# Slot table computed early, first group's chain reordered, bias added tile by tile, and constant matmuls on TensorE: an attention and mixture-of-experts kernel

## The chip, the cores and the metric

The kernel runs on one core of a Trainium2 chip. The metric is the device time of one execution in microseconds; lower is better. Engines are named as the profile names them: PE is TensorE (PEld its weight loads), DVE is VectorE, ACT is ScalarE, POOL is GpSimd, SP is the engine that issues most of the plain transfers.

## The reference

Input x has 16 sequences of 256 tokens with 128 features, in float32. All arithmetic is float32.

```python
x = x + attn(layernorm(x))      # 16 heads of 8; q and k divided by their norms; no softmax:
                                # out = (q k^T / 256**sigmoid(m)) v, then Wo and bo
x = x + ffn(layernorm(x))       # 8 experts, hidden size 512
# ffn: probs = softmax(x Wg^T); the two largest are taken
#      h = gelu(x w1[e] + b1[e]); eo = h w2[e] + b2[e]; out = sum of gate * eo over the two experts
```

## The kernel before

The 4096 tokens are 32 tiles of 128, in 8 groups of four tiles (`G = 4`, `NG = 8`); a group is two sequences. The kernel has three stages.

**Stage 1, attention and routing.** Every engine runs through `for n in STEPS` (n from -2 to 13) and calls a fixed, hand-written list of small functions, each for one group, such as `keys_of_x(n)` or `places(n - 2)`. Each engine works its list strictly in that order. A function begins with waits on semaphores and ends with an increment, so the lists mesh as a software pipeline. The life of group g:

- DVE takes statistics of x (`stats_of_x`, L832), ACT writes the normalised tile (`normalised`, L705), PE turns it (`turn_x`, L501), ACT copies it out (`turned_x`, L682), PE projects to q and k (`project`, L511). ACT squares them (`squares`, L694), DVE sums the squares (`sums_of_squares`, L881), clips them (`bounded`, L886), ACT takes the root (`norms`, L717), DVE inverts it (`inverse_norms`, L891) and scales q and k (`unit_qk`, L896).
- PE forms x^T k (`keys_of_x`, L529), ACT copies (`keys`, L699), PE multiplies by Wv (`values`, L545), DVE masks by heads (`heads`, L903), PE multiplies by Wo and by the router's weights (`out_weights` on PE, L552), ACT copies the product (`out_weights` on ACT, `gm`, L722), and PE applies it to q (`attend`, L561). DVE adds the residual (`attended`), whose bias part POOL wrote beforehand into `x2` (L443).
- DVE picks the two largest router values (`largest`, `where_largest`). PE counts how many earlier tokens go to each expert (`places` on PE, L570 to L574, into `psPos`, which shares a bank with the product `psGM`), DVE turns the counts into row numbers (`places` on DVE, L962 to L974), ACT writes the normalised rows (`rows`, L674). POOL scatters each tile twice with an indirect transfer into `xs` (L456), 64 transfers in all, in order of groups.

Step n of ACT begins with `out_weights(n - 2)`. PE's `places(n - 2)` waits for `s_gm >= n`, which means the copy of group n - 1. That copy is the first entry of ACT's step n + 1, behind `norms(n)`.

Between these, the expert weights are prepared, one expert per step: PE `centre_w1` (L474, L476), DVE `centred_w1` (L980), ACT `high_w1`, `high_w2` (L727, L732), DVE `low_w1`, `low_w2` (L985, L991).

After all steps PE sums the counts, DVE builds the table of slots (L1028 to L1048: which rows of `xs` each of 71 tiles of 128 rows starts at, and its expert), SP and ACT write eight blocks of padding (L337).

**Stage 2, experts.** A loop over 71 slots loads 128 rows (SP, L388 reads the row number into a register, L389 issues the load), turns them, runs both layers and scatters the results into `ys` (POOL, L463).

**Stage 3.** The two results of each token are read back, weighted and added to `x2`, and written out.

Of the kernel before, what the change touches and what calls it, by code (L numbers as in the profile page):

```python
# [19 lines left out]
P = 128  # L20
# [4 lines left out]
ALU = mybir.AluOpType  # L25
ACT = mybir.ActivationFunctionType
AX = mybir.AxisListType.X
# [4 lines left out]
def moe_block(nc, x, Wq, bq, Wk, bk, Wv, bv, Wo, bo, m, Wg, w1, b1, w2, b2, out, xs, ys):  # L32
# [8 lines left out]
    G = 4  # L41
# [17 lines left out]
    with ExitStack() as ctx:  # L59
# [284 lines left out]
        def _(sp):  # L344
# [32 lines left out]

            pads(sp, range(E // 2), s_pad)
            sp.wait_ge(s_tab, 1)
            sp.wait_ge(s_pad, 16 * (E // 2 + 1))  # L380
            sp.wait_ge(s_pad2, 16 * (E - E // 2))
# [4 lines left out]
            def load(s, b, i, e):  # L386
                after(sp, s_back[b], 16 * i)
                r = sp.value_load(rtab[0:1, bass.ds(s, 1)], min_val=0, max_val=E * REGION)  # L388
                sp.dma_start(xt[:, b, :], xs[bass.ds(r, P), :]).then_inc(s_xt[b], 16)  # L389
# [13 lines left out]
        def _(pool):  # L403
# [34 lines left out]
            for c in range(3):  # L438
                pool.wait_ge(s_xin[c], 16)
                n = G if c < 2 else NT - 2 * G  # L440
                t0 = c * G
                for q in range(t0, t0 + n, G):
                    pool.tensor_tensor(x2[:, q:q + G, :], xin[:, q:q + G, :],  # L443
                                       bobc[:].unsqueeze(1).to_broadcast([P, G, D]), ALU.add).then_inc(s_xb, 1)

# [25 lines left out]
        def _(pe):  # L471
            def centred(dst, src, bias):
# [4 lines left out]
                return mm  # L477

            pe.wait_ge(s_zero, 2)
            pe.wait_ge(s_const, 2)  # L480
# [7 lines left out]
            centred(psG[:, 0:E], wgT[:], None).then_inc(s_pw, 1)  # L488
            pe.wait_ge(s_w, 3)
            pe.wait_ge(s_ws, 3)  # L490
            pe.matmul(psKV[:, 0:E], woT[:], wgT[:], start=True, stop=True)
            pe.matmul(psKV[:, E:2 * E], borep[:], wgT[:], start=True, stop=True).then_inc(s_pw, 1)

            def turn_x(g):
# [82 lines left out]
            def centre_w1(e):  # L577
                if 0 <= e < E:
                    pe.wait_ge(s_wb, 32)
                    after(pe, s_w1, e)  # L580
                    centred(psQ[:], w1s[:, e, :], b1row[0:1, e, :]).then_inc(s_psW, 1)

            for n in STEPS:
                centre_w1(n - 3)
                out_weights(n - 1)
                turn_x(n + 1)
                places(n - 2)
                attend(n - 1)
                share_of_x(n)
                keys_of_x(n)  # L590
                project(n + 1)
                turn_q(n)
                values(n)

            pe.wait_ge(s_seen, NG)
            pe.wait_ge(s_pos, NG)
            pe.matmul(psCnt, ones[:, 0:1], seen[:], start=True, stop=True).then_inc(s_cnt, 1)


# [61 lines left out]
        def _(act):  # L661
# [130 lines left out]
        def _(dve):  # L792
# [195 lines left out]
            def low_w2(e):  # L988
                if 0 <= e < E:
                    dve.wait_ge(s_w2h, e + 1)  # L990
                    dve.tensor_tensor(w2p[:, e, :, 1, :], w2s[:, e, :].rearrange("p (c d) -> p c d", c=FC),  # L991
                                      w2p[:, e, :, 0, :].bitcast(F32), ALU.subtract).then_inc(s_w2l, 1)

            for n in STEPS:
                scale_and_shift(n - 1)
# [25 lines left out]
            links = [0]  # L1021

            def chain(ins):
                links[0] += 1
                ins.then_inc(s_tb, 1)
                dve.wait_ge(s_tb, links[0])
            dve.wait_ge(s_cnt, 1)
            dve.tensor_tensor(ptab[:], psCnt, regbase[0:1, 0, :], ALU.add).then_inc(s_ptab, 1)  # L1028
            chain(dve.tensor_scalar(cnti[:], psCnt, float(P - 1), None, ALU.add))
            chain(dve.tensor_scalar(tilesi[:], cnti[:], P.bit_length() - 1, None, ALU.logical_shift_right))  # L1030
            chain(dve.tensor_copy(tiles[:], tilesi[:]))
            dve.tensor_tensor_scan(tend[:], onee[:], tiles[:], 0.0, ALU.mult, ALU.add)
            chain(dve.tensor_scalar(tinc[:], tiles[:], -float(P), float(REGION), ALU.mult, ALU.add))
            chain(dve.tensor_tensor(past[:], sidx[:].unsqueeze(2).to_broadcast([1, NS, E]),
                                    tend[:].unsqueeze(1).to_broadcast([1, NS, E]), ALU.is_ge))
            dve.tensor_reduce(esum[:], past[:], AX, ALU.add)
            chain(dve.tensor_tensor(pinc[:], past[:], tinc[:].unsqueeze(1).to_broadcast([1, NS, E]), ALU.mult))
            dve.tensor_scalar(etabf[0:1, 1:1 + NS], esum[:], float(E - 1), None, ALU.min)
            chain(dve.tensor_reduce(rsum[:], pinc[:], AX, ALU.add))
            for half in range(2):  # L1040
                digits = etabf[0:1, half * HALF:half * HALF + NR * U].rearrange("p (i j) -> p i j", j=U)[:, :, 0:HALF]
                dve.tensor_tensor(eshift[:, :, half, :], digits,
                                  powers[:].unsqueeze(1).to_broadcast([1, NR, HALF]), ALU.mult)
            chain(dve.scalar_tensor_tensor(out=rsum[:], in0=sidx[:], scalar=float(P), in1=rsum[:],
                                           op0=ALU.mult, op1=ALU.add))
            with nc.allow_low_precision(reason="packed numbers below 2**15, summed in float32"):
                dve.tensor_reduce(ehalves, eshift[:], AX, ALU.add)
            dve.tensor_scalar(rtab[:], rsum[:], float(E * REGION), None, ALU.min).then_inc(s_tab, 1)  # L1048

# [91 lines left out]
```

## Time and profile before

| quantity | value |
|---|---|
| median of 3 runs | 326.46 us (326.45 to 327.78) |
| profiled execution | 326.04 us, span 324.1 us |
| PE busy | 249.6 us (77% of the span) |
| DVE busy | 208.8 us (64%) |
| ACT busy | 170.6 us (53%) |
| POOL busy | 147.6 us (46%) |
| stage 1 | from 0 to about 134 us |
| stage 2 | to about 300 us |
| stage 3 | to the end |

The profiled execution's own time is 1.94 us longer than its span, which runs from the first to the last instruction. Shares over the whole span mix three stages with different limits, so each stage has to be read by itself. The span and time of other kernels are to be compared with those of this one execution, and medians with medians.

### The profile page before, as it was taken

Reading aid. Unit: us, or ns where it says so; the run is one execution under the profiler, and the core shown is the slowest. Engines: PE = TensorE matmul, PEld = TensorE weight load, DVE = VectorE, ACT = ScalarE, POOL = GpSimd, SP = SyncE. Lnnn points to the kernel's source line nnn. Section 1 sums busy time; section 2 is a strip of 40 time slices with the busy share of each in tenths; the row PEclk is TensorE's granted clock in tenths of the full one; section 3 lists DMA queues with packets and bytes.
Section 4 is the critical chain, followed back from the end, with each engine's and each line's share of the span. In section 5 each row is a group of like instructions: output and inputs, shape, how many; then the busy total and the mean of one; then the engine's idle time right before and its main releaser. Section 6 shows DMA issues by size and latency. Waiting matters only on the chain.

```text
span 324.1 us, 6653 instructions
## 1 busy us (share of the span) xinstructions
PE 249.6 (77%) x1593; PEld 207.5 (64%) x1593; DVE 208.8 (64%) x788; ACT 170.6 (53%) x392; POOL 147.6 (46%) x172
## 2 busy tenths in 40 slices
PE   3847898899877650089999999999999999994000
PEld 1636677677754210069899989999898999894000
DVE  3475999979997659125665566556556655663385
ACT  4245576667754430345565556655655665562263
POOL 4380047776777777004344444444443444344000
PEclk9978999789997555569999999999999999999555
DMA  3798001111111112221212221212212222210897
GB/s 85 216 356 236 0 28 50 52 57 42 51 49 49 56 53 85 47 50 43 65 59 60 60 66 51 67 56 69 58 55 63 64 59 66 65 41 3 235 325 218
DMA packets 33643, 27.60 MB, mean 85 GB/s; under 512 B 4395, under 2 KB 28601, under 8 KB 33607
## 3 DMA queue, kind: packets, MB, share of 16 engines
q1 hardware_dynamic: 24344, 16.39, 18.2%
q0 software_dynamic: 4320, 8.43, 7.8%
q10 hardware_dynamic: 4944, 2.36, 2.6%
q8 instruction: 16, 0.26, 0.3%
q14 instruction: 19, 0.16, 0.2%
HBM read 16.05 MB, written 11.57 MB: 85 GB/s over the span
## 4 chain that ended last, share of the span: by engine, by line
PE 55%; DVE 19%; POOL 8%; DMA 7%; issue 5%; ACT 3%; SPq 2%; DVEq 0%; POOLq 0%; ACTq 0%
POOL xs L456 8%; PE psQK L615 6%; PE psQK L617 5%; PE psQK L616 5%; PE psG L634 5%; PE psQ L624 5%; PE psO L634 5%; PE psKV L624 5%; PE psG L637 4%; PE psO L637 4%; DMA w1s<-ys 4%; DVE n L881 3%; PE psQK L511 3%; DVE qk L896 2%; DVE n L891 2%
## 5 line engine op out<-in xcount | busy, mean ns | idle before, releaser
L463 POOL DMA_INDIRECT ys<-ring x71 | 68.9, 971 | 100.3 <-DVE ring L1082 98.2
L456 POOL DMA_INDIRECT xs<-row,slot x64 | 65.1, 1017 | 39.8 <-ACT row L674 22.2
L1070 DVE TENSOR_TENSOR hTl<-psQ,hTh 128x512 fp32r<-128x512 f32 x36 | 24.9, 691 | 30.3 <-ACT hTh L762 29.4
L770 ACT ACTIVATE ring<-psQK 128x512 f32<-128x512 f32 x71 | 42.9, 604 | 2.1 <-PE psQK L617 2.1
L1070 DVE TENSOR_TENSOR hTl<-psKV,hTh 128x512 fp32r<-128x512 f32 x35 | 24.2, 692 | 29.7 <-ACT hTh L762 29.7
L762 ACT CAST hTh<-psQ 128x512 fp32r<-128x512 f32 x36 | 21.1, 587 | 33.9 <-PE psQ L624 33.9
L762 ACT CAST hTh<-psKV 128x512 fp32r<-128x512 f32 x35 | 20.5, 587 | 30.3 <-PE psKV L624 30.3
L615 PE MATMUL psQK<-w1h,xTh 128*128 x71 | 34.9, 491 | 0.7 <-DVE xTl L1065 0.7
L617 PE MATMUL psQK<-w1h,xTl 128*128 x71 | 28.5, 402 | 0.0
L616 PE MATMUL psQK<-w1l,xTh 128*128 x71 | 28.5, 401 | 0.0
L634 PE MATMUL psO<-w2hl,hTh 128*128 x144 | 25.9, 302 | 0.6 <-DVE hTl L1070 0.6
L634 PE MATMUL psG<-w2hl,hTh 128*128 x140 | 25.1, 301 | 0.0
L609 PE MATMUL psX<-ident,ring 128*128 128x128 f32 x36 | 10.9, 302 | 17.1 <-DMA ring<-xs 17.1
L624 PE MATMUL psQ<-ident,ring 128*128 128x128 f32 x144 | 22.0, 276 | 0.3 <-ACT ring L770 0.3
L624 PEld LDWEIGHTS psQ<-ident,ring 128*128 128x128 f32 x144 | 18.2, 142 | 5.4 <-ACT ring L770 0.5
L624 PE MATMUL psKV<-ident,ring 128*128 128x128 f32 x140 | 21.0, 272 | 0.3 <-ACT ring L770 0.3
L624 PEld LDWEIGHTS psKV<-ident,ring 128*128 128x128 f32 x140 | 17.3, 140 | 5.3 <-ACT ring L770 0.7
L637 PE MATMUL psO<-w2hl,hTl 128*128 x144 | 20.2, 262 | 0.0
L634 PEld LDWEIGHTS psO<-w2hl,hTh 128*128 128x128 f32 x144 | 19.5, 190 | 0.8 <-issue 0.8
L637 PE MATMUL psG<-w2hl,hTl 128*128 x140 | 19.6, 262 | 0.0
L637 PEld LDWEIGHTS psO<-w2hl,hTl 128*128 128x128 f32 x144 | 19.0, 190 | 0.0
L634 PEld LDWEIGHTS psG<-w2hl,hTh 128*128 128x128 f32 x140 | 18.8, 189 | 0.0
(179 smaller groups left out, 574.8 us busy)
## 6 DMA issues: line engine op xcount, KB each, us to landing
ring<-xs SPq DMA_DIRECT2D x71, 64.5 KB, 1.9
w1s<-ys SPq DMA_DIRECT2D x16, 256.0 KB, 5.3
w1s<-in_L_ffn_w SPq DMA_DIRECT2D x1, 2048.0 KB
out<-x ACTq DMA_DIRECT2D x8, 256.0 KB, 4.8
ys<-ring POOLq DMA_INDIRECT x71, 2.2
xs<-row,slot POOLq DMA_INDIRECT x64, 2.3
xin<-in_L_attn_x SPq DMA_DIRECT2D x2, 256.0 KB, 3.5
b2bc<-in_L_ffn_b SPq DMA_DIRECT2D x1, 512.0 KB, 16.4
```

The source lines that it names most:

```text
L456: pool.indirect_dma_start(out=xs, out_offset=bass.IndirectOffsetOnAxis(ap=slot[:, p, j, k:k + 1], axis=0), in_=row[:, p, j, k, :], in_offs ...
L463: pool.indirect_dma_start(out=ys, out_offset=bass.IndirectOffsetOnAxis(ap=xt[:, b, D:ROW].bitcast(I32), axis=0), in_=y[:, b, :], in_offset ...
L609: pe.transpose(psXT[q], xt[:, b, 0:D], ident[:]).then_inc(s_psXT, 1)
L615: pe.matmul(psH[q], xTh[:, q, :], w1h[:, bass.ds(e, 1), :], start=True, stop=False)
L616: pe.matmul(psH[q], xTh[:, q, :], w1l[:, bass.ds(e, 1), :], start=False, stop=False)
L617: pe.matmul(psH[q], xTl[:, q, :], w1h[:, bass.ds(e, 1), :], start=False, stop=True).then_inc(s_psH, 1)
L624: mm = pe.transpose(psHT[q][:, c * P:(c + 1) * P], h[:, q, c * P:(c + 1) * P], ident[:])
L634: pe.matmul(psY[q], hTh[:, q, at], w2hl[:, bass.ds(e, 1), w:w + 2 * D], start=c == 0, stop=False)
L637: mm = pe.matmul(psY[q][:, 0:D], hTl[:, q, at], w2hl[:, bass.ds(e, 1), w:w + D], start=False, stop=c == FC - 1)
L762: act.copy(hTh[:, b % 2], psHT[b % 2][:]).then_inc(s_hTh, 1)
L770: act.activation(h[:, b % 2, :], psH[b % 2], ACT.Gelu).then_inc(s_h, 1)
L1070: dve.tensor_tensor(hTl[:, b % 2], psHT[b % 2][:], hTh[:, b % 2].bitcast(F32), ALU.subtract).then_inc(s_hTl, 1)
```

## The change

1. **Order of the steps.** PE calls `centre_w1` one step earlier and `places(n - 2)` ahead of `turn_x(n + 1)`. ACT calls `rows(n - 2)` between `turned_q` and `normalised`, where before it called `rows(n - 3)` near the head of the step, and `high_w1` one step earlier. DVE calls `places(n - 2)` ahead of `inverse_norms(n)`, and `centred_w1` and `low_w1` one step earlier.
2. **Router weight products.** The two small products with `wgT` (L491, L492) move behind `turn_x(0)`.
3. **Early table.** The count on PE and the slot table on DVE move into the step in which the last group has its places.
4. **SP** reads the row numbers of the first two slots as soon as the table is there, and only then waits for padding and scatters.
5. **POOL** adds the bias with one instruction per tile (32) where it had one per four tiles (8).
6. **Constant matmuls.** `keep_clock(n)` multiplies a constant bfloat16 matrix of ones by 512 columns of ones, n times, into a scratch bank: 7 times at the start, 10 times in step 0 ahead of `keys_of_x(0)`.

```diff
 # SP
+            def region_row(s):
+                return sp.value_load(rtab[0:1, bass.ds(s, 1)], min_val=0, max_val=E * REGION)
             sp.wait_ge(s_tab, 1)
+            first = [region_row(s) for s in range(2)]
             sp.wait_ge(s_pad, 16 * (E // 2 + 1))
...
-                r = sp.value_load(rtab[0:1, bass.ds(s, 1)], min_val=0, max_val=E * REGION)
+                r = first[s] if s < len(first) else region_row(s)
 # POOL
-                for q in range(t0, t0 + n, G):
-                    pool.tensor_tensor(x2[:, q:q + G, :], xin[:, q:q + G, :],
-                                       bobc[:].unsqueeze(1).to_broadcast([P, G, D]), ALU.add).then_inc(s_xb, 1)
+                for q in range(t0, t0 + n):
+                    pool.tensor_tensor(x2[:, q, :], xin[:, q, :], bobc[:], ALU.add).then_inc(s_xb, 1)
 # PE
+            def keep_clock(n):
+                for _ in range(n):
+                    pe.matmul(psQ[:], ones[:], ones[:].unsqueeze(1).to_broadcast([P, G, P]), start=True, stop=True)
+            pe.wait_ge(s_zero, 1)
+            keep_clock(7)
...
-            pe.wait_ge(s_w, 3)
-            pe.wait_ge(s_ws, 3)
-            pe.matmul(psKV[:, 0:E], woT[:], wgT[:], start=True, stop=True)
-            pe.matmul(psKV[:, E:2 * E], borep[:], wgT[:], start=True, stop=True).then_inc(s_pw, 1)
...
             for n in STEPS:
-                centre_w1(n - 3)
+                centre_w1(n - 2)
                 out_weights(n - 1)
+                places(n - 2)
                 turn_x(n + 1)
-                places(n - 2)
+                if n == -1:
+                    logit_weights()
+                if n - 2 == NG - 1:
+                    count()
                 attend(n - 1)
                 share_of_x(n)
+                if n == 0:
+                    keep_clock(10)
                 keys_of_x(n)
                 project(n + 1)
                 turn_q(n)
                 values(n)
-            pe.wait_ge(s_seen, NG)
-            pe.wait_ge(s_pos, NG)
-            pe.matmul(psCnt, ones[:, 0:1], seen[:], start=True, stop=True).then_inc(s_cnt, 1)
 # ACT
             for n in STEPS:
                 out_weights(n - 2)
-                rows(n - 3)
                 turned_x(n)
                 keys(n - 1)
                 high_w2(n - 3)
-                high_w1(n - 5)
+                high_w1(n - 4)
                 deviation(n - 1)
                 squares(n)
                 turned_q(n - 1)
+                rows(n - 2)
                 normalised(n + 1)
                 norms(n)
 # DVE
-                    dve.wait_ge(s_xb, g + 1)
+                    dve.wait_ge(s_xb, (g + 1) * G)
...
                 bounded(n)
+                places(n - 2)
                 inverse_norms(n)
-                places(n - 2)
                 unit_qk(n)
...
-                centred_w1(n - 3)
+                centred_w1(n - 2)
...
-                low_w1(n - 6)
+                low_w1(n - 5)
                 where_largest(n - 1)
+                if n - 2 == NG - 1:
+                    slot_table()
```

`count()` holds the three lines removed from PE's end, `logit_weights()` the four removed from its start, and `slot_table()` the table's instructions (L1028 to L1048) unchanged.

## Rows read from the trace of the kernel before

**Rows 1.** Timeline of POOL and DVE: start, duration, engine, line, idle before.

```profile
44.05 1.16 POOL L456 DMA_INDIRECT xs<-row,slot  x1 [19.45 <-ACT row L674]
...
76.07 0.97 POOL L456 DMA_INDIRECT xs<-row,slot  x1 [1.50 <-ACT row L674]
...
78.49 0.68 DVE L991 TENSOR_TENSOR w2hl<-w2s,w2hl 128x512 fp32r<-128x512 f32 x1
...
78.62 1.40 POOL L456 DMA_INDIRECT xs<-row,slot  x1 [0.30 <-issue]
...
118.16 0.97 POOL L456 DMA_INDIRECT xs<-row,slot  x1 [0.30 <-issue]
...
128.52 0.97 POOL L456 DMA_INDIRECT xs<-row,slot  x1 [0.30 <-issue]
```

**Rows 2.** Chain that ended last, 128 to 140 us: start, duration.

```profile
133.91 0.27 SPq L388
...
135.78 1.85 DMA ring<-xs
```

**Rows 3.** Waits of SP's queue: total us, times, longest.

```profile
SPq L384 <- DMA xs<-padrow: 4.6, 1, 4.6
```

**Rows 4.** Timeline of one step (n = 2), all engines.

```profile
38.41 1.65 ACT L705 ACTIVATE xn<-xin,shift,rstd 128x128 f32<-128x128 f32 x4
38.41 1.21 DVE L881 TENSOR_REDUCE n<-sq 128x128 f32<-128x1024 f32 x1
...
40.57 0.31 ACT L717 ACTIVATE nrm<-n 128x128 f32<-128x128 f32 x1 [0.50 <-DVE n L886]
40.78 0.37 ACT L722 COPY gm<-psG 128x272 f32<-128x272 f32 x1
...
41.05 2.07 ACT L674 ACTIVATE row<-x,shift,rstd 128x256 f32<-128x256 f32 x4
...
41.29 0.18 PE L570 MATMUL psG<-mask,tri 128*128 128x32 bf16 x1 [0.46 <-ACT gm L722]
...
41.78 0.13 DVE L962 TENSOR_TENSOR pos<-psG,regbase 128x32 f32<-128x32 f32 x1
...
42.41 1.22 DVE L896 TENSOR_TENSOR qk<-psQK,n 128x1024 f32<-128x1024 f32 x1
```

**Rows 5.** Timeline: the same two marks in later steps.

```profile
52.22 1.22 DVE L896 TENSOR_TENSOR qk<-psQK,n 128x1024 f32<-128x1024 f32 x1
...
58.04 1.65 ACT L705 ACTIVATE xn<-xin,shift,rstd 128x128 f32<-128x128 f32 x4
...
74.57 1.22 DVE L896 TENSOR_TENSOR qk<-psQK,n 128x1024 f32<-128x1024 f32 x1
...
80.86 1.65 ACT L705 ACTIVATE xn<-xin,shift,rstd 128x128 f32<-128x128 f32 x4
...
95.08 1.22 DVE L896 TENSOR_TENSOR qk<-psQK,n 128x1024 f32<-128x1024 f32 x1
```

**Rows 6.** Timeline of the first groups, 0 to 37 us.

```profile
13.07 3.75 PE L511 MATMUL psQK<-wqk,xnT 128*128 128x256 f32 x8 [0.68 <-ACT xnT L682]
...
17.22 7.38 POOL L443 TENSOR_TENSOR x<-xin,bobc 128x512 f32<-128x512 f32 x6 [5.87 <-DMA xin<-in_L_attn_x]
...
19.83 1.18 DVE L886 TENSOR_SCALAR n<-n 128x128 f32<-128x128 f32 x1
...
25.52 2.57 PE L511 MATMUL psQK<-wqk,xnT 128*128 128x256 f32 x8
...
35.10 1.89 PE L511 MATMUL psQK<-wqk,xnT 128*128 128x256 f32 x8
```

**Rows 7.** Timeline of PE in the first slot: two matmuls of 512 columns.

```profile
139.42 0.63 PE L616 MATMUL psQK<-w1l,xTh 128*128 x1
139.84 0.63 PE L617 MATMUL psQK<-w1h,xTl 128*128 x1
```

**Rows 8.** Windows of 10 us: PE, PEld, DVE, ACT, POOL busy, granted clock, DMA share, GB/s.

```profile
60.00:70.00 10.00, 9.12 (x48) 8.48 (x47) 7.98 (x44) 5.48 (x12) 7.56 (x9) 0.66 0.15 48
```

More of the change, by code:

```diff
@@ L581, in centre_w1, with count, logit_weights @@
                     centred(psQ[:], w1s[:, e, :], b1row[0:1, e, :]).then_inc(s_psW, 1)
+            def count():
+                pe.wait_ge(s_seen, NG)
+                pe.wait_ge(s_pos, NG)
+                pe.matmul(psCnt, ones[:, 0:1], seen[:], start=True, stop=True).then_inc(s_cnt, 1)
+            def logit_weights():
+                pe.wait_ge(s_w, 3)
+                pe.wait_ge(s_ws, 3)
+                pe.matmul(psKV[:, 0:E], woT[:], wgT[:], start=True, stop=True)
+                pe.matmul(psKV[:, E:2 * E], borep[:], wgT[:], start=True, stop=True).then_inc(s_pw, 1)
             for n in STEPS:
-                centre_w1(n - 3)
+                centre_w1(n - 2)
                 out_weights(n - 1)
+                places(n - 2)
                 turn_x(n + 1)
-                places(n - 2)
+                if n == -1:
+                    logit_weights()
+                if n - 2 == NG - 1:
+                    count()
                 attend(n - 1)
                 share_of_x(n)
+                if n == 0:
+                    keep_clock(10)
                 keys_of_x(n)
@@ L992, in low_w2, with slot_table, chain @@
                                       w2p[:, e, :, 0, :].bitcast(F32), ALU.subtract).then_inc(s_w2l, 1)
+            def slot_table():
+                links = [0]
+                def chain(ins):
+                    links[0] += 1
+                    ins.then_inc(s_tb, 1)
+                    dve.wait_ge(s_tb, links[0])
+                dve.wait_ge(s_cnt, 1)
+                dve.tensor_tensor(ptab[:], psCnt, regbase[0:1, 0, :], ALU.add).then_inc(s_ptab, 1)
+                chain(dve.tensor_scalar(cnti[:], psCnt, float(P - 1), None, ALU.add))
+                chain(dve.tensor_scalar(tilesi[:], cnti[:], P.bit_length() - 1, None, ALU.logical_shift_right))
+                chain(dve.tensor_copy(tiles[:], tilesi[:]))
+                dve.tensor_tensor_scan(tend[:], onee[:], tiles[:], 0.0, ALU.mult, ALU.add)
+                chain(dve.tensor_scalar(tinc[:], tiles[:], -float(P), float(REGION), ALU.mult, ALU.add))
+                chain(dve.tensor_tensor(past[:], sidx[:].unsqueeze(2).to_broadcast([1, NS, E]),
+                                        tend[:].unsqueeze(1).to_broadcast([1, NS, E]), ALU.is_ge))
+                dve.tensor_reduce(esum[:], past[:], AX, ALU.add)
+                chain(dve.tensor_tensor(pinc[:], past[:], tinc[:].unsqueeze(1).to_broadcast([1, NS, E]), ALU.mult))
+                dve.tensor_scalar(etabf[0:1, 1:1 + NS], esum[:], float(E - 1), None, ALU.min)
+                chain(dve.tensor_reduce(rsum[:], pinc[:], AX, ALU.add))
+                for half in range(2):
+                    digits = etabf[0:1, half * HALF:half * HALF + NR * U].rearrange("p (i j) -> p i j", j=U)[:, :, 0:HALF]
+                    dve.tensor_tensor(eshift[:, :, half, :], digits,
+                                      powers[:].unsqueeze(1).to_broadcast([1, NR, HALF]), ALU.mult)
+                chain(dve.scalar_tensor_tensor(out=rsum[:], in0=sidx[:], scalar=float(P), in1=rsum[:],
+                                               op0=ALU.mult, op1=ALU.add))
+                with nc.allow_low_precision(reason="packed numbers below 2**15, summed in float32"):
+                    dve.tensor_reduce(ehalves, eshift[:], AX, ALU.add)
+                dve.tensor_scalar(rtab[:], rsum[:], float(E * REGION), None, ALU.min).then_inc(s_tab, 1)
             for n in STEPS:
@@ L1017, in _ @@
                 variance(n)
-                low_w1(n - 6)
+                low_w1(n - 5)
                 where_largest(n - 1)
[L1021 to L1048, printed above, removed]
+                if n - 2 == NG - 1:
+                    slot_table()
             dve.tensor_tensor(dlog[:], bestall[:], bestall[:, :, 0:1].to_broadcast([P, NT, E]),
```

## The prediction

> **What bounds the kernel now.** I read the page's slices first: stage 2 keeps PE at 9 tenths, and nothing in it is edited, so the change can only move the time at which stage 2 starts, and what little stands around that. Next I followed the chain of waits back from there. The second load of stage 2 is issued at 135.78, and the chain comes from the last scatter, which starts at 128.52 and has landed just before SP's first register read at 133.91 [rows 1, 2]. SP's queue shows that the padding was as late: it waited 4.6 us for it and only 0.2 us more for the scatter [rows 3]. Before that POOL scatters without a break.
>
> So the second question is what paces POOL. In the timeline of POOL a scatter takes 0.97 us and 0.30 us of idle time, 1.276 us in all and 10.2 us for a group of eight. The first starts at 44.05, the last at 128.52 [rows 1]. POOL was not alone in setting that pace. At 76.07 it waited 1.50 us, 1.2 more than the usual gap, for ACT's rows of group 3 [rows 1]. The steps of the other engines are 9.6 to 10.6 us long, so they and POOL run almost in lock step. This is what the reader should see: an earlier first scatter helps only while the steps stay under 10.2 us.
>
> Third is the anatomy of a step [rows 4]. DVE is busy for 94% of it. DVE sums squares (38.41) and clips; ACT takes the root at 40.57 and copies `gm` at 40.78; PE's `places` follows at 41.29, and DVE's at 41.78. In the meantime DVE had been inverting the norms, and q and k follow at 42.41. The walk through ACT and PE costs DVE almost nothing, since the inversion (0.95 us) covers it.
>
> **The change, part by part.**
>
> *ACT's and DVE's new order (the large term).* Call A the time at which ACT is through with `turned_q` in step n; this is 38.41 for n = 2. Before, `normalised` (1.65) started there, and the root waited for DVE. Now `rows` goes first: 2.0 + 1.65 = 3.65 until the root can start, though DVE's input for it is there 2.1 after its sum. From the root to the end of the copy is 0.58 (40.57 to 41.15). From there to DVE's `places` it is 0.46 (0.14 to PE, 0.3 for its matmuls and the hand-over). DVE now stands in `places` ahead of `inverse_norms`; queued behind that wait are the inversion, q and k, and through these PE's keys and projection. `places` takes 0.63 and the inversion with its hand-over 0.99. So q and k start at A + 3.65 + 0.58 + 0.46 + 0.63 + 0.99 = A + 6.3, where they started at A + 4.0. DVE idles about 2.5 us where it had cover.
>
> From q and k to the next A it is 5.8 us (52.22 to 58.04) in steps 2 to 4, since `centred_w1` now comes in step 2 as well, and 6.3 us (74.57 to 80.86) in steps 5 and 6 [rows 5]. A step is then 12.1 us, later 12.6 us, against POOL's 10.2. Let T be the start of step 2's sum. A of steps 3 to 6 is T + 12.1, 24.2, 36.3 and 48.9; q and k of step 6 start at T + 55.2. Step 7 has no `normalised`, and DVE's sum starts 7.2 later (84.50 to 91.72 in the trace), the clip is done 1.5 after it, the root to `places` takes 1.05, and q and k 1.6 more: T + 66.5. Before it was 95.08 - 38.41 = 56.7 [rows 4, 5]. The reordering costs 9.8 us up to there, although the old number holds a stretch at the lower clock and the new one none.
>
> *POOL behind it.* Group 6's row numbers were complete 10.2 us after q and k of step 7. That gives T + 76.7, POOL's start T + 77.5 (0.8 from ready to start, as for group 3), group 7 at + 10.3, its last scatter 10.4 later as before [rows 1], so T + 98.2. Landing is 2.3 us, the median for these transfers, and not the 5.3 us of before, because the padding is no longer issued in the same microseconds: T + 100.5. For that, the count and the table must go early. They do: the table's 5 us and the padding, issued 2.6 us after its first value, lie beside the last eight scatters. The price if this cover is gone is the old 3 us.
>
> *Where T lies.* Rows of the first projection show PE at half speed: 3.75 us against 1.89 later [rows 6], 1.2 against 2.4 GHz, although the windows there report a granted clock of 1.00. I take a constant matmul at 0.42 us, the distance of two 512-column matmuls at half clock [rows 7]; as an upper bound the float32 centring matmuls of `w1` at that clock, 1.02 each, and as a lower one half of 0.42. Seven are 2.9 us from 2.3 to 5.3, hidden under the load that PE waits for until 5.34 (at the upper bound they would end at 9.5 and cost 4 us). If they lift the clock, the weight products end at 8.4; `turn_x(0)` waits for `normalised` (9.44) and ends at 10.1, ACT's copy at 10.75, with the two router products hidden under it; the projection ends at 12.7, not 16.8. But DVE's `stats_of_x(2)` stands ahead of `bounded(0)` and waits for the big load of x, which lands at 17.2 [rows 6]. This takes most of the gain: clip by 18.5, q and k from 19.9 to 21.1. The clip took 1.18 us where later ones take 0.21, held up by POOL's four-tile add [rows 6]; one-tile adds of 0.32 (a quarter of 1.26) up to perhaps 0.45 us hold it by no more than that. Ten constant matmuls after 17.3 last till 21.5 at the lower clock, 19.6 at the upper. I take 21.5. Keys and projection then take 2.9 us at full clock, ending at 24.4, against 28.1 (25.52 + 2.57). So T = 38.4 - 3.7 = 34.7. If the seven don't lift the clock, the projection ends at 16.4, the ten push the keys to about 24.5, and T = 37.6.
>
> *SP.* Between the scatters' landing and the second load there were 1.9 us (133.91 to 135.78), two register reads of about 0.7 each in them [rows 2]. With these done beforehand the second load leaves 0.5 us after landing: -1.4.
>
> *One-step shifts of the `w1` work* are the same 24 instructions elsewhere: nothing, beyond the 0.6 on DVE counted in step 2. *The 24 bias adds* end by 25.6 to 28, before `attended(0)` at about 31: hidden.
>
> *Long scatters.* Scatters of 1.3 to 1.5 us begin within 0.2 us after DVE's split of a weight, such as 78.62 behind 78.49 [rows 1]; seven of them cost 2.9 us in all. I keep their number, as the splits are as many: 0. The Trainium skill (SBUF — State Buffer, "Who interferes with whom") says that a `tensor_tensor` takes only the read side of the shared ports and so, as an inference, does not hold up GpSimd's descriptors. These rows speak against that. By that rule no scatter would be long on account of DVE; the sum would still not move.
>
> *Sum.* With T = 34.7 and a steady upper clock the landing is at 135.2, 1.4 later than 133.8, and SP gives 1.4 back: 0.0. Then the clock. In the old trace PE fell to half clock for some 7 us in 60 to 70 [rows 8], and that step took 12.3 us, 2 more than its neighbours. In the new step PE stands idle from the end of `out_weights` until `places`, some 2.7 us, in every step; an idle time of 2.6 us came before the fall at 20.5. Such a spell now makes `turn_x`, `attend` and `share_of_x` 4.9 us instead of 2.5, past q and k, and slows keys and part of the projection: 3.7 us. I take one: 326.04 + 3.7 = 329.7. The median of the runs shown stands 0.4 above the profiled execution, so 330.0.
>
> **The rivals.**
>
> *R1, the same within 0.5% (chance 0.18).* T as above and no spell, or a shorter wait of DVE: 326.4. For it speaks that the old trace has only one spell between 30 and 100 us; against it, the idle time now in each step.
>
> *R2, faster (0.19).* The steps stay under 10.2 us, because the hand-overs of root, copy and `places` overlap where I add them. Then POOL sets the pace from its first start: T + 5.4 + 0.8 = 41; 83.3 us to the last start (84.5 less the 1.2 of waiting), landing at 126.6, SP -1.4: about 318. It decides where DVE's sum comes less than 10.3 us after the sum before. Against it speaks the fixed order of ACT: rows and normalised take 3.65 before the root, whatever else is early.
>
> *R3, the constant matmuls do not lift the clock (inside the slower case, a third of it).* T = 37.6, and 332.6 with one spell, 336 with two.
>
> Slower by over 0.5% holds 0.63 altogether, with its own range 328.2 to 337.
>
> **How the numbers follow.** 0.5% is 1.6 us, about what a measurement of this kernel can tell from no change. The likeliest case is 330.0. Downwards the range reaches through R1 to a T earlier by 1 us without a spell, 325.0; R2 is left out. Upwards it goes to a cold head and nearly two spells, 335.5. That leaves out about 0.2.
>
> **What would show it.** First scatter at 40.5 to 44; DVE idle for about 2.5 us per step in front of `places`, released by PE; distance of two sums 12 to 13 us; POOL waiting 1.5 to 4 us for DVE's `slot` ahead of each group; last landing 2.3 us after its start; table and padding done before it. The prediction is wrong if POOL runs without gaps, or if PE keeps the upper clock throughout and the head comes earlier than 17.2 allows.

## The result, and the profile after

The changed kernel takes 340.12 us (median of 4 runs, 339.47 to 341.65), where the kernel before takes 326.49. The ratio is 1.044 with an interval of 1.037 to 1.051: slower, as predicted, but by 13.6 us where 3.5 were predicted, and outside the range of 325.0 to 335.5. The profiled execution took 340.42 us with a span of 338.7, so I compare its length with the 329.7 of the predicted sum: 10.7 us to be found.

One step of the changed kernel shows the predicted mechanism. Timeline of step 3, all engines; the step of before is in [rows 4].

```profile
51.97 1.21 DVE L897 TENSOR_REDUCE n<-sq 128x128 f32<-128x1024 f32 x1
52.04 2.08 ACT L690 ACTIVATE row<-x,shift,rstd 128x256 f32<-128x256 f32 x4
...
54.02 1.64 ACT L721 ACTIVATE xn<-xin,shift,rstd 128x128 f32<-128x128 f32 x4
55.56 0.30 ACT L733 ACTIVATE nrm<-n 128x128 f32<-128x128 f32 x1
55.76 0.37 ACT L738 COPY gm<-psG 128x272 f32<-128x272 f32 x1
56.27 0.18 PE L574 MATMUL psG<-mask,tri 128*128 128x32 bf16 x1 [2.21 <-ACT gm L738]
...
56.58 0.19 DVE L978 TENSOR_TENSOR pos<-psG,regbase 128x32 f32<-128x32 f32 x1 [2.50 <-PE psG L578]
...
58.25 1.22 DVE L912 TENSOR_TENSOR qk<-psQK,n 128x1024 f32<-128x1024 f32 x1
```

ACT writes the rows and then the normalised tile, the root comes 3.5 us after the rows began (55.56 - 52.04), `gm` behind it. PE is idle 2.21 us for that copy, DVE 2.50 us for PE. q and k start 6.2 us after the rows (58.25 - 52.04), where the prediction has 6.3. What I had counted once, the fall of the clock that such an idle time brings, comes in each of the five steps from T (the start of step 2's sum) to the sum of step 7. Windows of the same trace (window, length, then PE, PEld, DVE, ACT, POOL busy, granted clock, DMA share, GB/s):

```profile
40.00:50.00 10.00, 8.91 (x40) 8.41 (x41) 7.42 (x41) 2.62 (x8) 5.98 (x6) 0.50 0.10 33
51.00:56.00 5.00, 3.06 (x11) 1.29 (x9) 2.56 (x8) 5.00 (x12) 1.28 (x2) 1.00 0.09 28
57.00:63.00 6.00, 6.00 (x28) 5.82 (x27) 5.83 (x30) 1.36 (x3) 4.14 (x5) 0.50 0.11 34
64.00:70.00 6.00, 4.22 (x18) 2.32 (x16) 3.39 (x17) 5.19 (x12) 2.92 (x3) 1.00 0.13 44
71.00:74.00 3.00, 3.00 (x16) 3.00 (x14) 2.97 (x9) 0.00 (x0) 1.90 (x2) 0.50 0.09 27
...
98.00:104.00 6.00, 6.00 (x27) 5.82 (x26) 5.86 (x22) 1.48 (x4) 4.21 (x5) 0.50 0.11 38
```

The clock is read as a saw: a window at 1.00 (2.4 GHz) in which PE is busy 60 to 70% of the time, because it waits for `gm`, then one at 0.50 (1.2 GHz) in which PE is busy with hardly a pause. At the end of such a step DVE waits for PE's `values` (L549): 1.81 us up to 51.53, 0.85 up to 65.69, 0.44 up to 92.45. Between 40 and 104 us there are five such stretches (the one from 85 to 91 is not shown). The kernel before has one up to 101 us, from 61 to 67 [rows 8]; at 101 it falls again. The stretch at 71 to 74 is the shortest, and its step the only short one: the five steps take 15.1, 14.2, 12.6, 14.2 and 14.2 us. The Trainium skill (TensorE: Matmul & The Clock Gate, "HAM oscillation — how this bites in real kernels") describes such a saw for a kernel whose PE waits for transfers in each pass; the trace here shows one too, with waits of some 2.2 us for a copy of ACT.

The two ends of these five steps are DVE's sums at T and in step 7; POOL's timeline shows the first scatter, the start of the second group, a long scatter, and the last (compare [rows 1]):

```profile
36.86 1.21 DVE L897 TENSOR_REDUCE n<-sq 128x128 f32<-128x1024 f32 x1
...
107.05 1.21 DVE L897 TENSOR_REDUCE n<-sq 128x128 f32<-128x1024 f32 x1
```

```profile
42.50 1.17 POOL L459 DMA_INDIRECT xs<-row,slot  x1 [15.50 <-DVE row L990]
...
57.65 0.97 POOL L459 DMA_INDIRECT xs<-row,slot  x1 [5.06 <-DVE row L990]
...
138.64 4.15 POOL L459 DMA_INDIRECT xs<-row,slot  x1 [0.30 <-issue]
...
145.65 0.97 POOL L459 DMA_INDIRECT xs<-row,slot  x1 [0.30 <-issue]
```

POOL no longer scatters without a break: it waits 1.3 to 5.1 us ahead of each group from the second to the seventh. The chain that ended last goes through the last scatter as before (compare [rows 2]); its row shows the landing of 2.33 us, and the second load issued at 148.76:

```profile
145.65 2.33 DMA xs<-row,slot
...
148.76 2.10 DMA ring<-xs
...
150.91 0.49 PE psO L625
```

In SP's queue the scatters now end the wait, and the padding no longer shows (compare [rows 3]):

```profile
SPq L388 <- DMA xs<-row,slot: 8.5, 1, 8.5
```

The head, timeline of PE (compare [rows 6]):

```profile
2.31 3.17 PE L484 MATMUL psQ<-ones 128*128 128x512 bf16 x7 [2.31 <-POOL seen L420]
...
5.94 0.70 PE L477 MATMUL psQK<-wqk,negmean 128*128 128x256 f32 x2
...
9.58 1.08 PE L505 MATMUL psX<-ident,xn 128*128 128x128 f32 x4 [1.16 <-ACT xn L721]
...
11.34 3.78 PE L515 MATMUL psQK<-wqk,xnT 128*128 128x256 f32 x8
...
20.24 3.59 PE L484 MATMUL psQ<-ones 128*128 128x512 bf16 x10
...
24.56 1.89 PE L515 MATMUL psQK<-wqk,xnT 128*128 128x256 f32 x8
```

The seven constant matmuls do lift the clock: the weight products take 0.70 us, where they take 1.22 without constants (experiment 4). But PE then waits 1.16 us for the first normalised tile, and the first projection takes 3.78 us, as in the kernel before. The lift is used up before the work that it was to help.

### The profile page after: what moved, and what is told of

Read it like the earlier page. It is cut to its first block, busy times and chain, and to the rows that moved or that the text cites. A ratio compares the mean times of both kernels' runs of the same rounds, so it can differ in the third digit from the quotient of the medians.

```text
span 338.7 us, 6710 instructions
## 1 busy us (share of the span) xinstructions
PE 261.9 (77%) x1610; PEld 218.9 (65%) x1610; DVE 210.1 (62%) x788; ACT 169.7 (50%) x392; POOL 152.4 (45%) x196
## 4 chain that ended last, share of the span: by engine, by line
PE 64%; ACT 12%; POOL 7%; DVE 6%; DMA 6%; issue 5%; SPq 1%; POOLq 0%; DVEq 0%; ACTq 0%
PE psQK L631 6%; PE psQK L515 6%; POOL xs L459 5%; PE psQK L633 5%; PE psQK L632 5%; PE psG L650 5%; PE psQ L640 5%; PE psO L650 5%; PE psKV L640 5%; PE psG L653 4%; PE psO L653 4%; DMA w1s<-ys 4%; ACT row L690 3%; ACT xn L721 3%; PE psKV L533 3%
## 5 line engine op out<-in xcount | busy, mean ns | idle before, releaser
L459 POOL DMA_INDIRECT xs<-row,slot x64 | 66.5, 1039 | 53.2 <-DVE row L990 35.8
L625 PE MATMUL psX<-ident,ring 128*128 128x128 f32 x36 | 10.9, 303 | 18.8 <-DMA ring<-xs 18.8
L515 PE MATMUL psQK<-wqk,xnT 128*128 128x256 f32 x64 | 21.7, 501 | 0.0
```

The costliest lines, as they stand in the source:

```text
L459: pool.indirect_dma_start(out=xs, out_offset=bass.IndirectOffsetOnAxis(ap=slot[:, p, j, k:k + 1], axis=0), in_=row[:, p, j, k, :], in_offs ...
L515: mm = pe.matmul(psQK[:, j * 2 * D:(j + 1) * 2 * D], xnT[:, j, :], wqk[:], start=True, stop=True)
```

## The experiments

Each run is timed beside the kernel before on the same chip; ratios are against it. On two of the chips, called disturbed below, the kernel before took 345.71 and 346.76 us, and engines stood idle for microseconds with their inputs ready; the seven kernels timed there (e4 to e7, e15 to e17) are weak evidence, and I say so at each.

**1. All but the order, and the order alone.**

```diff
# e1_order_undone: the changed kernel with the order of before on PE, ACT and DVE
-                centre_w1(n - 2)
+                centre_w1(n - 3)
-                places(n - 2)          # PE: ahead of turn_x(n + 1)
+                places(n - 2)          # PE: behind it
-                rows(n - 2)            # ACT: ahead of normalised(n + 1)
+                rows(n - 3)            # ACT: behind out_weights(n - 2)
-                places(n - 2)          # DVE: ahead of inverse_norms(n)
+                places(n - 2)          # DVE: behind it
# likewise high_w1, centred_w1, low_w1 one step later
# e2_order_alone: the kernel before with the reverse of these lines and nothing else
```

> The changed kernel with its new order of steps taken back on PE, ACT and DVE (places, rows and the work on w1 stand where they stood), everything else of the change kept. Theory A, that the order makes the loop from ACT's root over PE's and DVE's places back to the inversion the bound of every step: steps return to 9.6 to 10.6 us, POOL scatters almost without gaps from about 42.5, the last scatter starts at 126 to 128, lands 2.3 us later since table and padding are early; 320 to 324 us. Theory B, that the constant matmuls leave PE's clock in a worse state for the rest of the stage: it stays at 333 or more. Theory C, that 32 bias adds on POOL hold up DVE at the head: first scatter no earlier than 44, and 326 or more.

> The kernel before with the new order of steps alone. Theory A: steps of 12 to 15 us as in the changed kernel, POOL waits 3 to 5 us for DVE's slot before most groups; 338 to 343 us. Theory B: 326 to 329 us, as there are no constant matmuls. Theory C: the same as B.

Measured: e1 325.52 us, ratio 0.995 (0.992 to 0.999); e2 339.36 us, 1.037 (1.031 to 1.043). The order by itself makes the loss: 12.4 us of 13.6. All the rest together is worth -1.4 us. From T on, the steps of e1 are 12.4 us once and 10.2 to 10.6 us otherwise. e1 lies 1.5 us above the 320 to 324 us expected for it; a scatter of 5.07 us, of which experiment 5 tells, stands in its trace.

**2. Which part of the order.** Each of these is the kernel before with one line moved.

```diff
# rows alone (ACT)
-                rows(n - 3)
+                rows(n - 2)            # between turned_q and normalised
# DVE's places alone
+                places(n - 2)
                 inverse_norms(n)
-                places(n - 2)
# PE's places alone
+                places(n - 2)
                 turn_x(n + 1)
-                places(n - 2)
```

On the disturbed chip first:

> The kernel before with ACT's rows alone moved ahead of normalised. Theory A with its parts added: the root starts 3.65 us after ACT is free and not 2.2, so q and k start at A + 5.5, 1.5 later than before and 0.8 earlier than with all three moves; steps of 11.3 to 12 us at the upper clock, still over POOL's 10.2: 332 to 338 us. If DVE's place ahead of the inversion is the whole cause, this one costs nothing: 325 to 328 us.

> The kernel before with DVE's places alone moved ahead of the inversion. Theory A: DVE waits 1.05 us behind the root instead of 0.35, q and k 0.8 us later per step, steps of 10.5 to 11.4 us, of which POOL's 10.2 hides a part: 328 to 331 us. If this is the whole cause of the changed kernel's slowness: 337 us or more.

> The kernel before with PE's places alone moved ahead of turn_x. Theory A: turn_x, attend and share_of_x come behind the copy of gm, the keys start up to 0.5 us later per step, and PE idles about 1.5 us more ahead of places: 326 to 330 us, the upper part if the lower clock comes more often.

Ratios 1.011 (1.005 to 1.017), 0.990 (0.982 to 0.997) and 1.016 (1.010 to 1.022): I drew nothing from them, and ran the same three kernels again on another chip.

> The kernel before with ACT's rows alone moved ahead of normalised, once more: on the chip of the first try the kernel before itself took 345.7 us, with engines idle although all they waited for was there. Theory A: 4 to 12 us slower than the kernel before on the same chip (steps of 11.3 to 12 us without a spell at the lower clock, 14 with one).

> The kernel before with DVE's places alone ahead of the inversion, once more for the same reason. Theory A: 0.8 us more per step, steps of 10.5 to 11.4 us at the upper clock: 1 to 6 us slower than the kernel before on the same chip.

> The kernel before with PE's places alone ahead of turn_x, once more. At the upper clock it costs at most 0.5 us per step: within 0.5% of the kernel before. If PE's idle time ahead of places brings spells at the lower clock, as the first try on the disturbed chip let it appear (steps of 14.5 us): 3 to 10 us slower.

| moved alone | us | ratio | steps from T on |
|---|---|---|---|
| ACT `rows` | 339.63 | 1.036 (1.029 to 1.043) | 15.0, 11.5, 13.4, 13.7, 13.7 |
| DVE `places` | 332.02 | 1.017 (1.014 to 1.020) | 12.2, 12.3, 11.0, 11.5, 11.6 |
| PE `places` | 325.67 | 1.001 (0.998 to 1.005) | 10.9, 10.3, 10.2, 10.6, 10.6 |

ACT's line alone costs as much as the whole reordering, 13.6 us beside the kernel before on its chip, which is more than the 4 to 12 expected. The other two came as expected, DVE's line 5.95 us slower (1 to 6 expected) and PE's the same. Timeline of step 2 with only ACT's line moved (e8):

```profile
38.38 2.08 ACT L674 ACTIVATE row<-x,shift,rstd 128x256 f32<-128x256 f32 x4
...
40.36 1.64 ACT L705 ACTIVATE xn<-xin,shift,rstd 128x128 f32<-128x128 f32 x4
41.90 0.30 ACT L717 ACTIVATE nrm<-n 128x128 f32<-128x128 f32 x1
42.09 0.37 ACT L722 COPY gm<-psG 128x272 f32<-128x272 f32 x1
42.14 1.09 PE L501 MATMUL psX<-ident,xn 128*128 128x128 f32 x4 [3.00 <-ACT xn L705]
42.23 0.95 DVE L891 RECIPROCAL n<-nrm 128x128 f32<-128x128 f32 x1 [1.74 <-ACT nrm L717]
...
43.40 0.19 DVE L962 TENSOR_TENSOR pos<-psG,regbase 128x32 f32<-128x32 f32 x1 [0.22 <-PE psG L574]
...
44.09 1.22 DVE L896 TENSOR_TENSOR qk<-psQK,n 128x1024 f32<-128x1024 f32 x1
```

q and k start 5.7 us after the rows began (44.09 - 38.38), where it was 4.0 before [rows 4]: the root is late, DVE idles 1.74 us for it, and PE stands idle 3.00 us, here for the normalised tile that `turn_x` needs and that ACT now writes behind the rows. DVE's line adds the uncovered inversion, up to the 6.3 of the prediction. With `rows` moved it seems to add nothing to the time (e2 339.4, e8 339.6), but e2 has PE's line and the `w1` shifts as well, and rows and DVE's line without those were not run together. PE's line costs nothing.

**3. The gap on PE filled.** The changed kernel, with nine constant matmuls in the place in which PE waits for `gm`:

```diff
                 out_weights(n - 1)
+                if group(n - 2) and n < NG:
+                    pe.wait_ge(s_qT, n)
+                    for _ in range(9):
+                        pe.matmul(psX[:], ones[:], ones[:].unsqueeze(1).to_broadcast([P, G, P]), start=True, stop=True)
                 places(n - 2)
```

> The changed kernel with nine more constant matmuls (into psX) between PE's out_weights and places in steps 2 to 7, where PE stood idle 2.5 us. If the idle time there is what takes PE to the lower clock: granted clock 1.00 from 25 to 110 us, steps of 12.1 to 12.6 us, as added up in the prediction, and 331 to 335 us. If the lower clock is not due to that idle time, or costs nothing on the path: 339 to 342 us, and if the added matmuls themselves delay places, more.

Measured: 334.61 us, ratio 1.025 (1.018 to 1.032), against 1.044 for the changed kernel. Timeline of PE, ACT and DVE in step 3, and three windows:

```profile
53.84 2.11 PE L604 MATMUL psX<-ones 128*128 128x512 bf16 x9
55.94 0.37 ACT L742 COPY gm<-psG 128x272 f32<-128x272 f32 x1
56.45 0.18 PE L574 MATMUL psG<-mask,tri 128*128 128x32 bf16 x1 [0.50 <-ACT gm L742]
...
56.76 0.19 DVE L982 TENSOR_TENSOR pos<-psG,regbase 128x32 f32<-128x32 f32 x1 [1.97 <-PE psG L578]
```

```profile
30.00:35.00 5.00, 4.54 (x22) 4.33 (x21) 4.13 (x15) 1.06 (x3) 0.00 (x0) 0.58 0.11 38
...
50.00:60.00 10.00, 8.86 (x53) 5.72 (x52) 7.93 (x39) 6.25 (x14) 6.55 (x7) 1.00 0.15 49
...
90.00:100.00 10.00, 8.64 (x60) 6.93 (x61) 7.70 (x27) 5.15 (x14) 5.76 (x7) 1.00 0.12 38
```

The wait for `gm` and DVE's idle time are still there; only PE's idle time is gone (0.50 instead of 2.21), and with it every stretch at the lower clock from 40 to 100 us. So the idle time makes the spells. The whole kernel is 5.5 us shorter, but this understates them. From T = 40.11 to the sum of step 7 at 102.47 it is 62.4 us, where the changed kernel needs 70.2: in these steps the spells cost 7.8 us, between 0.6 and 2.5 in each. Against this T comes 3.2 us later than in the changed kernel, since in this trace PE is at the lower clock from 31 to 37 us, ahead of the added matmuls (the first of them starts at 42.04); experiment 4 returns to that. What stays over the kernel before is 7.7 us. The chain is longer (62.4 us from T to the sum of step 7, 53.3 before), and one scatter takes 4.15 us. The prediction's own figures give 62.4 without a spell too (q and k of step 6 at T + 55.2, the sum 7.2 later). Its sum is met; its single steps are off by up to 0.9 us (12.6, 11.9, 12.0, 13.2 and 12.6 measured; 12.1 three times, 12.6 and 13.5 predicted).

**4. The constant matmuls of the head.** e12 is e1 without them.

```diff
-            keep_clock(7)
...
-                if n == 0:
-                    keep_clock(10)
```

> The version with the order undone (325.52 us, ratio 0.995) without the seven and ten constant matmuls. Theory A (as in the prediction): the constants lift the clock for the weight products and the first projection, so without them T is some 2 to 3 us later and the time is 327.5 to 329. Theory B: the clock had fallen again at 9.6 us in the changed kernel, so that the first projection took 3.78 us as before; the constants bring the head nothing, T stays at 36.5 to 37.5, and the time is 325.5 within 1 us. Theory C: the seven ahead of the weight products and the ten ahead of the keys only take time from PE, and the time is 324 to 325.

Measured: 323.8 us, ratio 0.995 (0.992 to 0.998), the same ratio as e1 with them. T is 36.85 in its trace, as in the changed kernel (36.86). Timeline of PE in the head:

```profile
5.81 1.22 PE L477 MATMUL psQK<-wqk,negmean 128*128 128x256 f32 x2
...
11.78 3.78 PE L514 MATMUL psQK<-wqk,xnT 128*128 128x256 f32 x8
...
23.38 3.16 PE L514 MATMUL psQK<-wqk,xnT 128*128 128x256 f32 x8
```

The weight products are slow again (1.22), the first projection is equally slow and starts 0.4 later, the second takes 3.16 instead of 1.89 and starts 1.2 earlier, since no constants stand ahead of it. In this pair of traces nothing is left at T. The traces of the other kernels say more, since their heads hardly differ from one of these; T in each, in us (runs on a disturbed chip in brackets):

| head | T |
|---|---|
| as before | before 38.41, e2 39.26, e8 38.38, e9 38.97, e10 38.83, (e4 38.62, e5 39.36, e6 38.69) |
| moved products, constants | changed 36.86, e1 36.02, e3 40.11, e11 40.94, e13 39.98, (e7 40.93) |
| moved products, no constants | e12 36.85, e14 37.20, (e15 37.55, e16 37.73, e17 37.27) |

With constants T is either 36 to 37 or 40 to 41 us. In the four late ones the granted clock is 0.50 from about 31 to 37 us, which no other trace here shows at that place. So the constants bring no gain at T, and in four of six traces a loss of some 3 us; with one execution each, how often is open. In the steps behind T this is in part made up, as e11 has no spell from 40 to 46 us where e1 and e12 have one.

Without constants T is 1.5 us earlier than the 38.41 of before, and the projection starts 1.3 us earlier than the 13.07 there [rows 6]. What the heads of e12 and the changed kernel share is the moved router products, for whose inputs PE waited ahead of the first turn before. This is the only other edit on PE up to there; it was not tried alone.

**5. The long scatter.** Behind the early table one scatter took 4.15 us in the changed kernel, 5.07 in e1 and e12. DVE's six last weight splits run back to back at that time (137.93 to 141.6 in the changed kernel). e7 is e1 with the table where the kernel before has it, e11 has it two steps later than e1, and e13 puts one split between each two instructions of the table's chain; e14 is e13 without constant matmuls.

```diff
# e11
-                if n - 2 == NG - 1:
+                if n - 4 == NG - 1:
                     slot_table()
# e13, e14 (the w1 work stays one step early, as in the changed kernel)
+                splits = [(f, e) for e in range(5, E) for f in (low_w2, low_w1)]
                 def chain(ins):
                     links[0] += 1
                     ins.then_inc(s_tb, 1)
+                    if splits:
+                        f, e = splits.pop(0)
+                        f(e)
                     dve.wait_ge(s_tb, links[0])
```

> The kernel with the order undone, with count and table moved back behind all steps. Theory D, that the scatter of 5.07 us there (and of 4.15 us in the changed kernel) stands still because the six splits of w1 and w2 on DVE, put behind the table, run back to back with all their inputs ready: the splits come ahead of the table again, no scatter takes over 1.6 us, the last one starts about 3.5 us earlier, but lands about 5 us later instead of 2.4, as the padding is late; within 1.5 us of the kernel with the order undone. Rival E, that the padding's transfers hold up POOL's queue: a scatter of 4 us or more remains, now behind the late padding.

> The kernel with the order undone, with DVE's slot table not in step 9 but in step 11, so that two of the three last pairs of splits of w1 and w2 come ahead of it and one behind. Theory D: no scatter over 2.2 us, the last scatter starts 3 us earlier than with the order undone, table and padding are still done before it: 318 to 322 us beside 326.5 for the kernel before. Rival E, that the padding's transfers hold POOL up: a scatter of 4 us or more remains.

> The order undone, except that the preparation of w1 stays one step early; the six last splits of w1 and w2 on DVE stand one each between the links of the table's chain instead of back to back behind it. Theory A (splits back to back hold up a scatter until their run ends): no scatter over 1.7 us, where the version with the order undone had one of 5.07; last scatter 3 to 4 us earlier than its 129.4; time 320 to 322.5, ratio 0.98 to 0.985. Theory B (something else behind the table holds the scatter, such as the padding): a scatter of 4 to 5 us stays, time 325 to 326.

> The same without constant matmuls. If they help the head (theory A of the run without them): 2 to 3 us longer than with them. If they bring nothing: within 1 us of it. Either way no scatter over 1.7 us.

| run | us | ratio | longest scatter, us |
|---|---|---|---|
| e7 (disturbed chip) | 346.35 | 0.998 (0.983 to 1.012) | 1.5 |
| e11 | 323.1 | 0.989 (0.986 to 0.992) | 2.34 |
| e13 | 324.97 | 0.995 (0.993 to 0.997) | 3.93 |
| e14 | 323.35 | 0.989 (0.987 to 0.991) | 4.53 |

e11 just missed its forecast (318 to 322 us, no scatter over 2.2). e13 and e14 missed theirs, no scatter over 1.7 us: with the splits apart the long scatter is still there, so it doesn't need them back to back. Timeline of POOL in e13, and of DVE beside it:

```profile
117.68 3.93 POOL L459 DMA_INDIRECT xs<-row,slot  x1 [0.30 <-issue]
121.91 1.48 POOL L459 DMA_INDIRECT xs<-row,slot  x1 [0.30 <-issue]
```

```profile
117.94 0.67 DVE L1007 TENSOR_TENSOR w2hl<-w2s,w2hl 128x512 fp32r<-128x512 f32 x1
118.55 0.15 DVE L1026 TENSOR_TENSOR_SCAN tend<-onee,tiles 1x8 f32<-1x8 f32 x1
...
118.70 0.67 DVE L1001 TENSOR_TENSOR w1l<-w1s,w1h 128x512 fp32r<-128x512 f32 x1
119.30 0.73 DVE L1028 TENSOR_TENSOR xin<-sidx,tend 1x568 f32<-1x568 f32 x1
...
120.56 0.72 DVE L1030 TENSOR_REDUCE esum<-xin 1x71 f32<-1x568 f32 x1
```

DVE itself has no gap there, as the table's instructions fill the places between the splits. The rival, the padding, can't have started the hold: SP issues its four blocks at 119.29 to 121.20, ACT its four from 119.2, and the scatter had begun at 117.68. Three more kernels, on the second disturbed chip: e15 is e12 with one-input instructions that write zeros in the place of the six last splits (it leaves the low parts of these experts' weights out of the result), and e16 and e17 move the table without the constants (as e11 and as e7).

> The version with the order undone and without constants (323.8 us, one scatter of 5.07). In place of the six last splits (experts 5 to 7) one-input instructions of the same size write zeros, so the low parts of these experts' weights are left out of the result. Theory A (an unbroken run of instructions that read two tiles of SBUF holds up a scatter): no scatter over 1.4 us behind the table, last scatter some 4 us earlier, time 320 to 321.5. Theory B (what holds it is not the second input: any run from SBUF, or something else that comes with the early table): a scatter of over 3 us stays. Theory C (the scatter isn't the end that counts): no long scatter, and the time stays at 323.8.

> The order undone, no constants, and the slot table two steps later. If the constants bring nothing and the table's place is worth what it was with them (ratio 0.9892 against 0.9951): no scatter over 2.4 us and 321.5 to 323, ratio 0.985 to 0.99. If the gain of the later table was a difference between chips: 323.8 as with the early table.

> The same with the table where the kernel before has it, behind all steps. What is left of the change is then the moved router weight products, the bias tile by tile and SP's two early readings. No scatter over 1.6 us. If the padding ends the wait for stage 2 as in the kernel before (4.6 us of it seen there), the earlier scatters bring nothing and the time is 325 to 326.5; if not, 321 to 323.

Measured: e15 340.0 us, 0.983 (0.976 to 0.990); e16 342.32, 0.978 (0.969 to 0.988); e17 345.41, 0.988 (0.978 to 0.997). On that chip the ratios are worth little, but what one scatter does beside DVE can be read. In e15 a scatter of 3.75 us stays; e16, with the table two steps later, has none over 1.50. In e17, where the splits run back to back from 139.54 to 143.83 ahead of the table, the scatters beside them are these:

```profile
139.61 1.46 POOL L459 DMA_INDIRECT xs<-row,slot  x1 [0.30 <-issue]
141.38 1.50 POOL L459 DMA_INDIRECT xs<-row,slot  x1 [0.30 <-issue]
143.18 1.50 POOL L459 DMA_INDIRECT xs<-row,slot  x1 [0.30 <-issue]
```

So neither the two inputs of the splits nor their standing back to back is enough; the same splits cost 0.5 us a scatter ahead of the table and 3 to 4 us in one scatter behind it. e15 changes more than the number of inputs: its instructions take 0.41 us each where a split takes 0.67, so it shows only that the long scatter comes without the six splits, and not which property of DVE's work matters. Wherever the table's last links and the splits came ahead of the two instructions on `bestall` and `rall` with no gap, the scatter ended 0.4 us after these (143.83 against 143.44 in e15; 142.79 against 142.40 in the changed kernel). The 2.34 of e11 ends so as well (130.86 against 130.48); e13's and e14's end earlier, inside the table's chain. What holds it is open.

## Why the prediction was right or wrong

**Right: direction, mechanism and place.** ACT's `rows` ahead of the root, PE's wait for `gm`, DVE's uncovered inversion and POOL's waits came as written, and e2, e8 and e9 put the loss there. The predicted length of the steps without a spell, 62.4 us from T to the sum of step 7, is what e3 shows, though its single steps are off both ways. The landing of 2.3 us and the padding out of the way were right too. R2 fell with the fixed order of ACT, R1 with DVE's full wait and the spells.

**The step that failed: "I take one" spell of the lower clock, 3.7 us.** The same paragraph said that the idle time is there in every step, and the sum took its spell once. From T to the sum of step 7 the changed kernel needs 70.2 us (107.05 - 36.86) where 62.4 + 3.7 = 66.1 were forecast: +4.1. Against e3's 62.4 its spells, one in each of the five steps, cost 7.8 us, 1.6 each on average. So the number of spells was too low and the price of one too high, and the two errors hid each other in part: five at 3.7 would have been 18.5. This term alone would have put the time at 334.1, still inside the range; with T it is outside.

**T: 34.7 predicted, 36.86 measured, +2.2.** The step was that the seven constant matmuls keep the clock up for the first projection. They lift it for the weight products, a wait of PE follows, and the projection takes 3.78 us and not 1.9. R3, which put T at 37.6, was the nearer case, and its reason, a first projection at half clock, is what came; e12 shows the constants to be worth nothing in the end. R3 with two spells, 336, is also the figure nearest to the result, but that is luck: two at 3.7 make 7.4, where five short ones made 7.8.

**The end of stage 1: +2.8.** From the sum of step 7 to the last scatter it is 38.6 us (145.65 - 107.05) against 35.8 forecast (98.2 - 62.4). The step "I keep their number: 0" for the long scatters missed the one of 4.15 us, 3.2 above the usual 0.97. The Trainium skill (SBUF — State Buffer, "Who interferes with whom") infers that a `tensor_tensor` does not hold up GpSimd's descriptors; these traces speak against it as the prediction's rows did: scatters beside a split take 1.3 to 1.5 us, 0.97 elsewhere. What decides the long one is open, as experiment 5 tells.

**SP: 0.5 less than forecast.** From landing to the first work on the second load it is 2.93 us (147.98 to 150.91); before it was 3.85 (133.83 to 137.68). That is a gain of 0.9, not 1.4: the load leaves 0.8 us after the landing and not 0.5, and takes 2.10 us where it took 1.85.

**Stage 3: 1.25 us, not in the sum.** From its first load of results to the end it took 25.4 us (313.31 to 338.7), before 24.15 (299.95 to 324.1). No edit touches it. 1.0 of it is in the two transfers on its path that read results back: 5.65 and 7.06 us, before 5.36 and 6.31. It doesn't follow the change: the same stretch takes 23.6 us in e3, which is the changed kernel with matmuls added, and 25.5 in e9. What moves it is open.

Together 2.2 + 4.1 + 2.8 + 0.5 + 1.25 = 10.85. The execution is 1.7 us longer than its span, where 1.94 was taken over from before, which leaves 10.6 of the 10.7 us to be found.

The parts taken one at a time by medians are 12.4 for the order and -1.4 for the rest, 11.0, where the two together gave 13.6. The intervals of the ratios (1.031 to 1.043 and 0.992 to 0.999, against 1.037 to 1.051) allow this without an interaction, and they don't exclude one.

Two versions come out 1.1% faster than the kernel before: the order undone with the table two steps later (323.1, ratio 0.989), and the one without constants with the splits between the table's links (323.35, 0.989). Their intervals lie apart from 1, but not apart from each other. e1, e12 and e13 follow at 0.995, each with an interval just below 1.

## What to carry to other kernels

When a new wait puts idle time on PE in every pass of a loop, price the lower clock in every pass: count the passes, then look for a reason to leave one out. Take the price from a step that had a spell; here a spell cost 0.6 to 2.5 us and not 3.7. Before an entry is moved ahead in a hand-written order, ask what else stands behind it on the same engine; here two microseconds of rows, put ahead of a root of 0.3 us that two engines wait for, cost 13 us, and moving the wait on PE cost nothing. Constant matmuls paid here where they stood in the idle time itself: there they gave back 5.5 us. At the start, where PE waited again between them and the work that they were for, they gave back nothing.

## What the hardware showed that I had not expected

- PE idle times of 2.2 us per step went with stretches of 3 to 10 us at 0.50 in each of five steps; with constant matmuls in the gap the clock stayed at 1.00 from 40 to 100 us.
- In the head the granted clock and the durations don't agree: in the kernel before the windows show 1.00 where eight matmuls take 3.75 us [rows 6], and 1.89 later; I went by the durations of equal matmuls there.
- Constant matmuls ahead of the first groups left T at 36 to 37 us in two traces and put it at 40 to 41 in four, with the clock at 0.50 from about 31 to 37 us; without them it was 36.9 to 37.7 in five.
- One indirect scatter took 3.75 to 5.07 us on POOL beside DVE work that costs its neighbours some 0.6 us at most, and it did so in seven kernels with the early table, at either spacing of the weight splits.
- The bias added by tiles took 9.93 us for 24 tiles, 0.41 each, where the kernel before took 7.38 us for the same tiles in six instructions [rows 6]: a third more, and hidden in both.
